# Causal 16-head attention on one core: each corner's mask as one 128-row product instead of four 32-row ones

## What is computed

```python
def _L1_attn_ref(x, W_Q, W_K, W_V, W_O):           # x is layer-normed; 16 heads of 8
    Q, K, V = (proj(W_Q), proj(W_K), proj(W_V))    # (4, 16, 1024, 8)
    Q = _apply_rope(Q, cos, sin)
    K = _apply_rope(K, cos, sin)
    scores = jnp.einsum('bhsd,bhtd->bhst', Q, K) / jnp.sqrt(jnp.float32(D_K))
    causal = jnp.tril(jnp.ones((S, S), dtype=bool))
    scores = jnp.where(causal[None, None], scores, -jnp.inf)
    attn = jax.nn.softmax(scores, axis=-1)
    out = jnp.einsum('bhst,bhtd->bhsd', attn, V)
    return jnp.einsum('bsd,ed->bse', out, W_O)
```

## Time and profile before

| | |
|---|---|
| median of 3 runs | 5059.8 us (5048.36 to 5063.59) |
| the profiled execution | 5060.94 us, span 5059.6 us |
| PE busy over the span | 4684.2 us, 93% |
| DVE, ACT busy | 4358.4 us (86%), 3294.9 us (65%) |
| mean granted clock | 0.967 |

### The profile page before, as it was taken

The page is one execution under the profiler, slowest core; times in us unless marked ns, Lnnn a source line. Parts: engine busy times, 40 slices in busy tenths (PEclk is TensorE's granted clock), DMA queues, the critical chain, the costliest instruction groups (busy, mean ns, idle before and its releaser), DMA issues.

```text
span 5059.6 us, 146025 instructions
## 1 busy us (share of the span) xinstructions
PE 4684.2 (93%) x60680; PEld 3208.4 (63%) x60680; DVE 4358.4 (86%) x9139; ACT 3294.9 (65%) x6490; POOL 2933.2 (58%) x3101
## 2 busy tenths in 40 slices
PE   6999997999999999999999999999996999989978
PEld 3333333777777777777777777777775555545467
DVE  7999997999999999999999999999995777768566
ACT  3888885666666666666666666666663677756632
POOL 1320303878877887788778877877782222016644
PEclk7999998999999999999999999999996999979989
DMA  0000100000000000000000000000000000000000
GB/s 24 1 1 1 33 5 25 23 10 12 13 27 10 12 13 27 10 12 13 27 11 12 13 27 11 19 13 10 8 5 27 2 2 2 2 16 1 1 1 17
DMA packets 51751, 63.48 MB, mean 13 GB/s; under 512 B 12820, under 2 KB 41258, under 8 KB 50322
## 3 DMA queue, kind: packets, MB, share of 16 engines
q1 hardware_dynamic: 51090, 54.14, 3.6%
HBM read 25.17 MB, written 4.19 MB: 6 GB/s over the span
## 4 chain that ended last, share of the span: by engine, by line
PE 53%; DVE 28%; issue 8%; ACT 8%; POOL 2%; DMA 0%; DVEq 0%; SPq 0%; POOLq 0%; ACTq 0%
PE psum L558 7%; PE psum L1220 6%; PE psum L1158 6%; PE psum L529 6%; PE psum L1203 4%; DVE a_top L707 4%; PE psum L1235 3%; PE psum L1275 3%; DVE b_cross L1474 3%; PE psum L1167 3%; DVE b_stat L1513 3%; DVE x L1507 2%; DVE x L1470 2%; PE psum L545 2%; DVE b_prob_t L1526 1%
## 5 line engine op out<-in xcount | busy, mean ns | idle before, releaser
L1627 POOL TENSOR_TENSOR x<-x,b_cross 128x512 f32<-128x512 f32 x768 | 985.7, 1287 | 58.5 <-DVE b_cross L1474 58.5
L1633 POOL TENSOR_TENSOR x<-x,b_norm 128x512 f32<-128x512 f32 x768 | 789.4, 1048 | 210.1 <-ACT b_norm L1314 208.4
L1235 PE MATMUL psum<-b_w_vo,b_mixed 128*128 128x128 f32 x6144 | 778.1, 275 | 0.0
L1235 PEld LDWEIGHTS psum<-b_w_vo,b_mixed 128*128 128x128 f32 x6144 | 752.2, 192 | 26.5
L707 DVE TENSOR_REDUCE a_top<-psum 128x1 f32<-128x512 f32 x1024 | 643.1, 682 | 62.6 <-PE psum L529 58.5
L641 ACT ACTIVATE a_prob<-psum 128x512 f32<-128x512 f32 x1024 | 558.3, 604 | 106.1 <-PE psum L545 97.3
L1640 POOL TENSOR_TENSOR x<-x,b_stat 128x512 f32<-128x512 f32 x384 | 398.2, 1051 | 303.4 <-DVE b_stat L1518 303.2
L1307 ACT ACTIVATE b_square<-psum 128x512 f32<-128x512 f32 x768 | 462.4, 602 | 143.1 <-PE psum L1158 120.3
L1356 ACT COPY b_mixed<-psum 128x512 f32<-128x512 f32 x768 | 439.3, 600 | 142.4 <-PE psum L1220 142.4
L1470 DVE TENSOR_TENSOR x<-psum,b_table 128x512 f32<-128x512 f32 x768 | 514.3, 670 | 18.8 <-ACT b_square L1307 18.3
L1474 DVE TENSOR_TENSOR b_cross<-psum,b_table 128x512 f32<-128x512 f32 x768 | 520.2, 677 | 0.0
(11 more groups left out here) (354 smaller groups left out, 10733.5 us busy)
## 6 DMA issues: line engine op xcount, KB each, us to landing
b_prev<-b_xs_x SPq DMA_DIRECT2D x24, 384.0 KB
ab<-in_L_ffn_Wqkv SPq DMA_DIRECT2D x6, 1024.0 KB, 5.2
b_shifted_x<-y SPq DMA_DIRECT2D x24, 224.0 KB
b_shifted_f<-y SPq DMA_DIRECT2D x48, 112.0 KB, 2.1
ab<-in_L_ffn_Wqkv SPq DMA_DIRECT2D x6, 512.0 KB, 6.1
ab<-in_L_ffn_Wo SPq DMA_DIRECT2D x6, 512.0 KB, 7.3
b_prev<-b_xs_x SPq DMA_DIRECT2D x24, 112.0 KB
x<-in_L_attn_x SPq DMA_DIRECT2D x4, 512.0 KB, 6.9
```

Source lines behind the costliest of these rows:

```text
L1235: made = e.matmul(banks[n][:, 0:D], mixed[:, h, :], w_vo[l % 2][:, h, :], start=h == 0, stop=h == 2 * PAIRS - 1)
L1627: e.tensor_tensor(turned, turned, crossing, ALU.add).then_inc(sem["roped"], 1)
L1633: e.tensor_tensor(rh, rh, bcast(norm[i % 2][:, 1, HPC * c:HPC * (c + 1)], 2, LDIM), ALU.mult).then_inc(sem["scaled"], 1)
```

## The change

Each corner's four 32-row products become one product over all 128 rows, the whole identity `ident_bf` against a whole triangle in `chip.masks`, both already on the chip for other stages. It carries no `tile_position`. The constant `c_blocks`, its load, its cast, and the waits on them go.

```diff
-        blocks = sb("blocks", [3, 4, P], BF16) if causal else None
@@ sync_
-            if causal:
-                nc.sync.dma_start(blocks_f, ins["c_blocks"]).then_inc(sem["dma_blocks"], 16)
@@ tensor_, first
                     if corner:
-                        q.wait_ge(sem["blocks_cast"], 1)
-                        for m in range(4):
-                            e.matmul(banks[n][:, wide - P + ROWS * m:wide], blocks[part, 0, m, :],
-                                     blocks[part, 1, m, ROWS * m:P], start=m == 0, stop=False,
-                                     skip_group_check=True, tile_position=(ROWS * head, 0))
+                        q.wait_ge(chip.constants_cast, 2)
+                        e.matmul(banks[n][:, wide - P:wide], chip.ident_bf[:, :], chip.masks[:, 0:P], start=True, stop=False,
+                                 skip_group_check=True)
@@ tensor_, second
                     if diagonal(c, k):
-                        q.wait_ge(sem["blocks_cast"], 1)
-                        for m in (3, 2, 1, 0):
-                            e.matmul(banks[n][:, lo:lo + ROWS * (m + 1)], blocks[rows_of, 0, m, :],
-                                     blocks[rows_of, 2, m, 0:ROWS * (m + 1)], start=m == 3, stop=False,
-                                     skip_group_check=True, tile_position=(ROWS * g, 0))
+                        q.wait_ge(chip.constants_cast, 2)
+                        e.matmul(banks[n][:, lo:lo + P], chip.ident_bf[:, :], chip.masks[:, P:2 * P], start=True, stop=False,
+                                 skip_group_check=True)
@@ vector_, weights
-                    if causal:
-                        q.wait_ge(sem["dma_blocks"], 16)
-                        e.tensor_copy(blocks[:, :, :, :].rearrange("p n m q -> p (n m q)"),
-                                      blocks_f).then_inc(sem["blocks_cast"], 1)
```

More of the change, by code:

```diff
@@ L375, in mha_stage @@
     sem = chip.semaphores(name, "dma_weights dma_bias cleared top_cleared normed rotated biased zeroed k_split q_split "
-                                "v_copied rounded topped raised shifted valued finished dma_blocks blocks_cast")
+                                "v_copied rounded topped raised shifted valued finished")
     with ExitStack() as scope:
@@ L394, in mha_stage @@
             qkv, turn1, xn = sb("qkv", [TILES, 3 * D]), sb("turn1", [TILES, 2 * D]), moe.yn
-        blocks_f = turn1[:, 0:6, :].rearrange("p t d -> p (t d)")
         turn2 = chip.y[:, 0:2 * TILES, :].rearrange("p (t s) d -> p t (s d)", t=TILES)
@@ L2404, in mask_constants @@
     return np.concatenate([np.eye(P), causal_qk, causal_qk.T, usual, opening, numbers], 1).astype(np.float32)
[L2407 to L2411, removed]
 def constants():
     small, local = rotary_constants()
-    return dict(c_small=small, c_local=local, c_masks=mask_constants(), c_blocks=block_constants())
+    return dict(c_small=small, c_local=local, c_masks=mask_constants())
 def build(nc, ins, out, stages="ABCD"):
```

## The result

The changed kernel takes 5813.52 us (median of 4 runs, 5790.79 to 5819.43) against 5058.22 us (4 runs) for the kernel before: a ratio of 1.15, interval 1.1479 to 1.1522. The profiled span is 5813.2 us, 753.6 us longer than before. Later comparisons have more runs of the kernel before beside them, 5053 to 5054 us.

The account below looks back on a forecast made before the run. PE was taken to bound stage c. At mostly 1.2 GHz, units 2 to 14 add 595 us, and units 0, 1, 15 and the end bring it to 696 over 5060.9: 5757, predicted as 5750, range 5400 to 5860.

Parts of the forecast that it names:

- The bound: Stage c's passes, units 2 to 14: PE is what everything waits for, idle only 0.9 us of 34.2 a unit.
- The change of shape: At each full mask in stage c the array runs empty twice; each step costs its length minus 0.07 us.
- The sum at full clock: Stage c at 2.4 GHz: 18.3 us a unit more, 17.4 after idle PE, 278 us over 16 units.
- The clock: PE enters stage c's passes at 1.2 GHz and mostly stays there, as drains thin its work; 5650 to 5860 us, chance 0.62.
- The unit: One unit of stage c's passes at 1.2 GHz: components of 82.4 us, taken as 80, against 34.2 before.
- The four slots without a corner: Slots of a stage c unit with no masks, priced at 0.73 us each at 1.2 GHz.
- The twelve slots with four corners: Slots of a stage c unit with four full masks, at 0.75 us a corner, 3.00 us each at 1.2 GHz.
- units 0, 1 and 15 and the end: Rest of stage c's passes: 5, 38 and 48 us more, and 10 for the lone second pass at the end.
- The head of stage c: Start of stage c: the removed 768 KB load and 0.95 us cast are hidden, gaining 0, at most 0.95 us.
- A high clock: Rival: the clock stays high through most of stage c's passes; 5339 us, or 5300 to 5400, chance 0.14.
- The switching clock: Rival: half of each stage c unit at either clock level, about 66 us a unit; 5570 us, chance 0.20.
- The faster rival: Rival: the array does not run empty around a full mask in stage c, so fewer instructions win; 5010 us, chance 0.03.

Follow-up runs that it names:

- the run with eight masks: Every full mask of the changed kernel issued eight times in a row, the first seven overwritten; 5731.52 us, ratio 1.1346 to the kernel before.

## Why the prediction was right

**The bound.** PE bound stage c with 0.9 us of idle time a unit, and the added steps came out nearly whole: DVE and ACT have the same work in 2.5 times the time.

**The change of shape** was right in kind and size. The mask's step, taken from a 32-row mask, was 0.155 us; measured 0.16 at 2.4 GHz, and 0.21 to 0.22 against 0.21 at 1.2. The sum at full clock gave 18.3 us a unit more, of which up to 0.9 hidden; the run with eight masks gives 18.7.

**The clock** was right: 3.4 us into the passes it was down to 0.5, it rose six times for 3 to 14 us and once more at the very end, and was down for nearly all of the passes. I took it from two places in the trace of before, where it rose and where it fell, two places only, and the chance of 0.62 allowed for that. The 0.50 at a busy 3893.1 to 3906.8, which the prediction counts as agreement, shows only that a PE that is busy 12.3 of 13.7 us can stay at 1.2 GHz; it does not show what would release the clock. What bears out the link to how densely PE streams came afterwards: with eight masks there is more work in less time. Nearly the same instructions at 64.0 and 40.2 us in one run show what the clock costs, and also that a unit's instructions alone do not settle at which level it runs.

**The unit** was 4.7 us too small: the components came to 82.4, I took 80, and 84.7 was measured. The 2.4 us taken off for moments at full clock were about right: the clock was up for 34 us of the 1101.4, in five rises, and at 84.7 to 52.9 us of work that saves some 1.6 us a unit (an estimate). So the components, all at 1.2 GHz, are what was short, by some 3.9 us. A unit with the clock down throughout shows where:

```profile
4079.10:4162.10 83.00, 82.30 (x290) 35.94 (x289) 27.31 (x55) 27.11 (x56) 0.00 (x0) 0.50 0.00 1
...
4137.75 0.79 PE L523 MATMUL psum<-c_kt,c_q 32*128 32x512 f32 x2
4139.33 0.79 PE L523 MATMUL psum<-c_kt,c_q 32*128 32x512 f32 x1 [0.35 <-DVE c_top L693]
4140.06 1.94 PE L550 MATMUL psum<-c_prob,c_v 128*32 128x512 f32 x8
```

The four slots without a corner were priced at 0.73 us, the length of one product. They stand in pairs with nothing between them, and the second slot's last first product starts only at 4139.33, when DVE has emptied its bank: two slots take 2.31 us (4137.75 to 4140.06), so 1.7 us more a unit. The wait of 0.35 us stood already in the earlier trace rows. The twelve slots with four corners took 3.16 us in the mean, not 3.00, another 1.9 us: 512 columns are more frequent in them than one in four, and the product behind a mask is longer than I took it. I used the mean of products most of which follow others of their own shape (450 and 781 ns for 128 and 512 columns), and behind a mask they take 471 and 790 (groups by shape in one unit, 4162.1 to 4246.0 us):

```profile
L537 PE MATMUL psum<-c_q,c_kt 32*128 32x512 f32 x24 | 12.7, 790 | 0.0
...
L523 PE MATMUL psum<-c_kt,c_q 32*128 32x128 f32 x9 | 4.2, 471 | 0.0
```

At about 0.02 us and 64 corners that is some 1.3 us of a unit, most of it in these twelve slots. Thirteen units at 84.7 in place of 80 are 61 us, about the distance from 5750 to 5813; units 0, 1 and 15 and the end, priced at 101 us together, came to 101 (1346.7 less 588.9 and 656.7).

**The head of stage c** was priced at 0 to 0.95 us gained. From POOL's last addition of stage b to the projection it took 15.7 us before (3851.77 to 3867.51) and 14.5 now (3849.55 to 3864.00). The chain is the norm, which is not touched; one profile of each doesn't tell whether this is the change.

**The rivals.** A high clock, 5339, did not happen, but the run with eight masks shows what it would have been: 52.9 us a unit. The switching clock, 5570, did not happen here, with 34 of 1101.4 us at the high level; with full masks in one pass alone, or four at a time, it did. The faster rival, without a drain, is refuted by every pair of steps in the timeline. Its estimate of 48 us takes all four small masks at the least length of a product; they are 128, 96, 64 and 32 columns wide, so it was no estimate of them.

## What to carry to other kernels

Before replacing several small products by a larger one, look at which part of the array the neighbours use: if the large one has another shape, each switch can set strips that ran side by side one behind the other, as it did here. If it must be, put all products of one shape together; the same full masks cost 755 us singly, 88 in pairs and 15 in fours. And price a change that thins PE's work out at both clock levels, with the rows that the trace has at each: here the clock took more than the switches.

## What was not expected

Eight full masks a corner were faster than one, though four were slower: 5813.5 us with one, 5905.1 with four, 5731.5 with eight. And only reordering the small masks across strips shortened the path from a slot's first mask to its last product, from 0.39 us to 0.28 in the slots shown, and won 0.27% of the whole.
